# SwitchHead attention in a four-layer Trainium2 kernel: keys in four partition groups, probabilities turned by VectorE, gated values halved by GpSimd

## The reference, cut to what matters

```python
q = _rope(jnp.einsum('bsd,hdp->bhsp', x, Wq))        # 16 heads of 64
k = _rope(jnp.einsum('bsd,hdp->bhsp', x, Wk))
gv = _gate(x, Wsel_v)                                # 2 of 8 experts, sigmoid weights
v = jnp.einsum('bsd,bhse,hedp->bhsp', x, gv, Wv)
att = jax.nn.softmax(jnp.einsum('bhsp,bhtp->bhst', q, k) / np.sqrt(P), axis=-1)
o = jnp.einsum('bhst,bhtp->bhsp', att, v)
go = _gate(x, Wsel_o)
src2 = jnp.einsum('bhsp,bhse,hepd->bsd', o, go, Wo)
```

## Time and profile before

| | |
|---|---|
| median of 3 runs | 5357.71 us (5347.48 to 5360.96) |
| the profiled execution | 5350.9 us |
| its span, first to last instruction | 5349.1 us |
| mean granted TensorE clock | 0.966 |
| SwitchHead's score rows | 1062.5 to 3645.7 us of the span |

### The profile page before, as it was taken

The page is one execution under the profiler, slowest core; times in us unless marked ns, Lnnn a source line. Parts: engine busy times, 40 slices in busy tenths (PEclk is TensorE's granted clock), DMA queues, the critical chain, the costliest instruction groups (busy, mean ns, idle before and its releaser), DMA issues.

```text
span 5349.1 us, 83763 instructions
## 1 busy us (share of the span) xinstructions
PE 4801.0 (90%) x30340; PEld 2480.0 (46%) x30378; DVE 3571.9 (67%) x4077; ACT 2898.9 (54%) x3797; POOL 2348.7 (44%) x1499
## 2 busy tenths in 40 slices
PE   6989898689999999999999999997888988888856
PEld 2334333256556666565666556564333322222226
DVE  5899999866655565556655674654776778888721
ACT  5665556245445545555455554553555557667743
POOL 4888888535534543535534444443221221120014
PEclk8999999899999999999999999998999999999978
DMA  4555555323332332333323332233112101101005
GB/s 152 189 182 183 179 190 193 124 56 82 86 80 78 86 94 72 82 83 79 94 68 86 89 95 65 72 91 85 39 34 43 41 25 26 25 25 25 2 30 169
DMA packets 202377, 467.59 MB, mean 87 GB/s; under 512 B 35179, under 2 KB 52078, under 8 KB 201316
## 3 DMA queue, kind: packets, MB, share of 16 engines
q1 hardware_dynamic: 198968, 455.89, 29.9%
q0 software_dynamic: 3008, 6.32, 0.3%
HBM read 417.51 MB, written 33.99 MB: 84 GB/s over the span
## 4 chain that ended last, share of the span: by engine, by line
PE 72%; issue 9%; DVE 8%; ACT 6%; POOL 3%; DMA 0%; SPq 0%; POOLq 0%; DVEq 0%; ACTq 0%
PE ps L2258 8%; PE ps L1350 8%; PE ps L1370 8%; PE ps L1389 8%; PE ps L1358 7%; PE ps L1339 7%; PE ps L548 4%; PE ps L2229 3%; PE ps L2211 3%; ACT n_P L2293 3%; PE ps L495 2%; PE ps L1332 2%; DVE ps L713 1%; DVE n_MX L2372 1%; DVE m_HH L734 1%
## 5 line engine op out<-in xcount | busy, mean ns | idle before, releaser
L2372 DVE TENSOR_REDUCE n_MX<-ps 128x2 f32<-128x1024 f32 (+6 forms) x1034 | 982.2, 979 | 235.6 <-PE ps L2211 137.1
L1496 ACT ACTIVATE s_P<-ps,s_MX 128x1024 f32<-128x1024 f32 x512 | 570.4, 1114 | 968.1 <-DVE s_MX L1660 968.0
L2293 ACT ACTIVATE n_P<-ps 128x1024 f32<-128x1024 f32 (+4 forms) x1022 | 825.3, 838 | 447.2 <-PE ps L2229 233.7
L1652 DVE TENSOR_TENSOR XTB<-ps,s_GVJ 128x1024 f32<-128x1024 f32 x256 | 313.2, 1223 | 837.3 <-PE ps L1339 836.4
L771 POOL TENSOR_TENSOR m_PR<-m_HH,m_CS 128x1024 f32<-128x1024 f32 x256 | 605.9, 2381 | 156.2 <-issue 129.4
L1660 DVE TENSOR_REDUCE s_MX<-ps 128x1 f32<-128x1024 f32 x512 | 600.3, 1214 | 32.1 <-PE ps L1350 32.0
L1867 POOL TENSOR_TENSOR s_OG<-s_OG,s_OT 128x1024 f32<-128x1024 f32 x256 | 604.4, 2374 | 38.8 <-DMA s_OG<-s_gt 38.6
L1505 ACT ACTIVATE shared<-ps 128x1024 f32<-128x1024 f32 x512 | 496.7, 1023 | 140.0 <-PE ps L1358 138.4
L1350 PE MATMUL ps<-s_QF 64*128 64x512 f32 x2048 | 510.6, 617 | 28.1 <-POOL s_QF L1859 20.0
L1358 PEld LDWEIGHTS ps<-ident,s_P 128*128 128x128 f32 x4096 | 464.0, 141 | 150.5 <-issue 135.3
L1370 PEld LDWEIGHTS ps<-shared,s_V 128*64 128x64 f32 x8192 | 442.0, 137 | 197.4 <-issue 172.4
(11 more groups left out here) (352 smaller groups left out, 6484.7 us busy)
## 6 DMA issues: line engine op xcount, KB each, us to landing
m_CS<-m_rows_c SPq DMA_DIRECT2D x256, 512.0 KB
s_OG<-s_gt SPq DMA_DIRECT2D x512, 256.0 KB, 4.2
m_BS<-m_rows_c SPq DMA_DIRECT2D x80, 512.0 KB
s_WV<-in_s_v SPq DMA_DIRECT2D x32, 512.0 KB, 4.0
s_TA<-XTB SPq DMA_DIRECT2D x256, 64.0 KB, 2.3
s_WO<-in_s_o SPq DMA_DIRECT2D x32, 512.0 KB, 5.3
g_WB<-in_g_wx SPq DMA_DIRECT2D x23, 578.0 KB
n_parts<-n_PT SPq DMA_DIRECT2D x14, 768.0 KB, 3.4
```

The lines of the kernel that those rows point to most:

```text
L2293: ins = s.activation(P[:, at:at + x.shape[1], lo:512], x[:, :, lo:512], ACT.Exp, scale=scale)
L2372: ins = v.tensor_reduce(self.MX[:, q, at:at + x.shape[1], hp, t], x[:, :, 0:width], AX.X, ALU.max)
```

## The change

Scores are laid out anew. A tile's score block (128 queries x 1024 keys) becomes 32 matmuls in place of 4: for query group a (32 queries) and key group x (keys whose index has (k mod 128) // 32 = x), the result of 32 x 256 goes to partitions 32x to 32x+31 and columns 256a. With keys in the partitions' groups this way, a transpose in blocks of 32x32 is all that the probabilities need, and VectorE does it from SBUF to SBUF (`v.transpose`, 128x1024), in place of TensorE's transposes and ScalarE's copies.

A query's maximum and sum are then spread over four partition groups. ScalarE copies the scores to SBUF (`row`); VectorE takes maxima of 256 (`max`); SP gathers the four groups with four DMAs; VectorE reduces over them (`most`); SP sends the result to the four groups with four more; ScalarE takes eight exponentials of 256 columns per tile in place of two of 1024 (`exp`). At the end of a half SP gathers the sums with four DMAs, VectorE adds, inverts and transposes them (`recip`), SP stores them to DRAM (`spread`) and broadcasts them back with two DMAs (`over`), and GpSimd multiplies as before. The steps `turn` and `sums` leave TensorE and the ring of PSUM slots.

The sum over the 8 gated experts is split: GpSimd adds the upper four to the lower four (512 elements), and VectorE adds up the four that are left in a step of its own, `v_sum`, later in the turn. In a turn the order is now: gated, onto, recip, max, v (product, halving), exp of the tile before, its first transpose, most, its second transpose, v_sum, sums, spread, over, collect, values, keep, rope, ahead, qk, gate_in.

```diff
     NG = 3
-    NP = 4
+    NP = 6
...
-        self.MX, self.M1 = sb("MX", [128, 8]), sb("M1", [128, 64])
-        self.SU, self.SR, self.SX = sb("SU", [128, 2, 4, 2]), sb("SR", [128, 2, 4, 2]), sb("SX", [128, 4, 2, 64])
+        self.M1 = sb("M1", [128, 64])
+        self.MX, self.MB = sb("MX", [128, 2, 8]), sb("MB", [128, 2, 8])
+        self.MG, self.MR = sb("MG", [32, 2, 4, 8]), sb("MR", [32, 2, 8])
+        self.SU, self.SG, self.SR = sb("SU", [128, 2, 32]), sb("SG", [32, 4, 32]), sb("SR", [32, 3, 32])
...
-        self.PT = [self.TMP[:, u * 2048:(u + 1) * 2048].rearrange("p (h k n) -> p h k n", h=2, k=NT) for u in range(2)]
+        self.PT = [self.TMP[:, u * 2048:(u + 1) * 2048].rearrange("p (h n) -> p h n", h=2) for u in range(2)]
...
+        if m % 4 == 1 and due(5):
+            out.append(("recip", *self.of_half(m // 4 - 1)))
+        if due(0):
+            out.append(("max", *tile(0)))
+        if m == 2:
+            next(vs)
+            out.append(("v_sum", *out[-1][1:]))
+            begun = len(out)
+        next(vs, None)
+        if due(1):
+            out.extend([("exp", *tile(1), 0), ("exp", *tile(1), 1), ("turn", *tile(1), 0)])
+        if due(0):
+            out.append(("most", *tile(0)))
+        if due(1):
+            out.append(("turn", *tile(1), 1))
+        out.extend(("v_sum", *s[1:]) for s in [s for s in out[begun:] if s[0] == "v"])
+        if m % 4 == 0 and due(4):
+            out.append(("sums", *self.of_half(m // 4 - 1)))
+        if m % 4 == 1 and due(5):
+            out.append(("spread", *self.of_half(m // 4 - 1)))
+        if m % 4 == 2 and due(6):
+            out.append(("over", *self.of_half(m // 4 - 1)))
+        if due(self.GATED + 1) and part(self.GATED + 1)[1] == 3:
+            out.append(("collect", *self.of_half(part(self.GATED + 1)[0])))
+        if due(2):
+            g = m - 2
+            out.append(("values", *self.pair(g // 8), g % 8))
+            if g % 4 == 3:
+                out.append(("keep", *self.of_half(g // 4)))
...
-        if m % 4 == 0 and due(4):
-            out.append(("recip", *self.of_half(m // 4 - 1)))
-        for _ in range(2 if m == 2 else 1):
-            next(vs, None)
...
+            elif kind == "max":
+                g = self.tile(*step[1:])
+                sp.wait_ge(self.mx_done, g + 1)
...
+                for x in range(4):
+                    sp.dma_start(self.MG[:, g % 2, x, :], self.MX[32 * x:32 * x + 32, g % 2, :]).then_inc(self.mg_in, 16)
+            elif kind == "most":
+                g = self.tile(*step[1:])
+                sp.wait_ge(self.most_done, g + 1)
...
+                for x in range(4):
+                    sp.dma_start(self.MB[32 * x:32 * x + 32, g % 2, :], self.MR[:, g % 2, :]).then_inc(self.mb_in, 16)
+            elif kind == "sums":
+                k = self.half(*step[1:])
+                sp.wait_ge(self.exp_done, 8 * (k + 1))
...
+                for x in range(4):
+                    sp.dma_start(self.SG[:, x, :], self.SU[32 * x:32 * x + 32, k % 2, :]).then_inc(self.su_in, 16)
+            elif kind == "spread":
+                k = self.half(*step[1:])
+                sp.wait_ge(self.recip_done, 2 * (k + 1))
...
+                sp.dma_start(self.sums_d[k % 2], self.SR[:, 2, :]).then_inc(self.sums_out, 16)
+            elif kind == "over":
+                k = self.half(*step[1:])
+                sp.wait_ge(self.sums_out, 16 * (k + 1))
...
+                rows = self.sums_d[k % 2].rearrange("(t h a) q -> h t (a q)", t=4, h=2)
+                for h in range(2):
+                    sp.dma_start(self.OR[k % 2][64 * h:64 * h + 64, 1, :].rearrange("p (t n) -> p t n", t=4),
+                                 rows[h].partition_broadcast(64)).then_inc(self.or_in, 16)
...
-                for q in chunks(L):
-                    for h in range(2):
-                        hs = slice(64 * h, 64 * h + 64)
-                        ins = pe.matmul(r.ap(two[h])[:, q], QF[hs, 0, t * 128:(t + 1) * 128], QF[hs, 1, q], start=True, stop=True)
-                        if q.stop == L:
-                            ins.then_inc(*r.fill(two[h]))
-            elif kind == "turn":
-                P = self.P[self.head(step) % self.NP]
-                r.taken(pe, ("row", *step[1:]))
-                r.empty(pe, step)
-                for t in range(NT):
-                    ins = pe.transpose(ps[:, t * 128:(t + 1) * 128], P[:, t * 128:(t + 1) * 128], c.ident[:, :])
-                ins.then_inc(*r.fill(step))
...
+                        place = self.O[64 * h:64 * h + 64, 128 * (g % 4):128 * (g % 4) + 128].rearrange("p (a n) -> p a n", n=32)
+                        P = self.PT[g % 2][:, h, :].rearrange("p (a k n) -> p a k n", a=4, n=32)[:, :, i, :]
+                        ins = pe.matmul(place, self.V[j % 2][:, h, i, :], P, start=i == 0, stop=i == NT - 1)
...
             elif kind == "row":
-                g, x = self.tile(*step[1:4]), self.head(step)
-                s.wait_ge(self.mx_done, x + 1)
+                x = self.head(step)
+                r.filled(s, step)
                 if x >= self.NP:
-                    r.filled(s, self.old("turn", x - self.NP))
-                if g % 4 == 0 and g >= 8:
-                    s.wait_ge(self.recip_done, g // 4 - 1)
-                s.activation(self.P[x % self.NP][:, :], ps, ACT.Exp, bias=self.MX[:, x % 8:x % 8 + 1],
-                             accum_out=self.SU[:, g // 4 % 2, g % 4, step[4]:step[4] + 1]).then_inc(*r.take(step))
-            elif kind == "turn":
...
-                s.activation(self.PT[g % 2][:, step[4], :, :].rearrange("p k n -> p (k n)"), ps, ACT.Copy).then_inc(*r.take(step))
+                    s.wait_ge(self.pt_done, x - self.NP + 1)
+                s.activation(self.P[x % self.NP][:, :], ps, ACT.Copy).then_inc(*r.take(step))
+            elif kind == "exp":
+                g, x, h = self.tile(*step[1:4]), self.head(step), step[4]
+                if h == 0:
+                    s.wait_ge(self.mb_in, 64 * (g + 1))
+                    if g % 4 == 0 and g >= 8:
+                        s.wait_ge(self.su_in, 64 * (g // 4 - 1))
+                for a in range(4):
+                    P, at = self.P[x % self.NP][:, 256 * a:256 * a + 256], 8 * (g % 4) + 4 * h + a
+                    ins = s.activation(P, P, ACT.Exp, bias=self.MB[:, g % 2, 4 * h + a:4 * h + a + 1],
+                                       accum_out=self.SU[:, g // 4 % 2, at:at + 1])
+                ins.then_inc(self.exp_done, 1)
...
-                r.taken(v, step)
-                v.tensor_reduce(self.V[u][:, :, t, :], four(self.VP), AX.X, ALU.add).then_inc(self.v_done, 1)
-            elif kind == "row":
-                x = self.head(step)
-                r.filled(v, step)
-                if x >= 8:
-                    r.taken(v, self.old("row", x - 8))
-                v.tensor_reduce(self.MX[:, x % 8:x % 8 + 1], ps, AX.X, ALU.max, negate=True).then_inc(self.mx_done, 1)
+            elif kind == "max":
+                g = self.tile(*step[1:])
+                if g > 1:
+                    v.wait_ge(self.mg_in, 64 * (g - 1))
+                for h in range(2):
+                    x = self.head((*step, h))
+                    r.taken(v, ("row", *step[1:], h))
+                    ins = v.tensor_reduce(self.MX[:, g % 2, 4 * h:4 * h + 4],
+                                          self.P[x % self.NP][:, :].rearrange("p (a k) -> p a k", a=4), AX.X, ALU.max)
+                ins.then_inc(self.mx_done, 1)
+            elif kind == "v_sum":
+                t, u = step[3], j % 2
+                VP = self.VP.rearrange("p (h q e) -> p h q e", h=2, e=8)
+                v.wait_ge(self.halved, n(*step))
+                v.tensor_reduce(self.V[u][:, :, t, :], VP[:, :, :, 0:4], AX.X, ALU.add).then_inc(self.v_done, 1)
+            elif kind == "most":
+                g = self.tile(*step[1:])
+                v.wait_ge(self.mg_in, 64 * (g + 1))
+                if g > 1:
+                    v.wait_ge(self.mb_in, 64 * (g - 1))
+                v.tensor_reduce(self.MR[:, g % 2, :], self.MG[:, g % 2, :, :].rearrange("p x e -> p e x"), AX.X, ALU.max,
+                                negate=True).then_inc(self.most_done, 1)
+            elif kind == "turn":
+                g, x = self.tile(*step[1:4]), self.head(step)
+                v.wait_ge(self.exp_done, x + 1)
+                if g == 0:
+                    v.wait_ge(self.top_done, 1)
+                elif g > 1:
+                    v.wait_ge(self.values_done, g - 1)
+                v.transpose(self.PT[g % 2][:, step[4], :], self.P[x % self.NP][:, :]).then_inc(self.pt_done, 1)
             elif kind == "recip":
                 k = self.half(*step[1:])
...
-                v.reciprocal(self.SR[:, k % 2, :, :], self.SU[:, k % 2, :, :]).then_inc(self.recip_done, 1)
+                v.wait_ge(self.su_in, 64 * (k + 1))
```

(21 more changed lines are left out.)

99 lines of the change are left out of this document (47 added, 52 removed).

## The result

The changed kernel takes 5779.2 us (median of 4 runs, 5777.7 to 5789.4), the kernel before 5359.3 us beside it. The ratio is 1.079 with an interval of 1.077 to 1.081: 420 us slower, where 71 us slower were forecast. The profiled execution has a span of 5778.5 us.

A forecast was written before the change was run, and what follows sets the result against it. TensorE bounds the kernel before; after the change SP's queue would set the round, 10.05 us plus extras, 10.4 against 10.1. Over 256 turns +77 us; 5350.9 + 77 + 7 gives 5435, rounded to 5430; range 5160 to 5650.

The forecast's parts named there:

- The mechanism forecast first: SwitchHead's score stage: SP's issues and the trip inside its queue eat what the transposes gave; 5370 to 5530, chance 0.50.
- The rival of cheap issues: SP's small copies cost 0.3 us an issue, so TensorE binds with 8.6 to 9 us a turn; 5050 us, chance 0.13.
- that of dear transposes: An engine is dearer: VectorE block transposes of 2.44 us or scores at 3.8, a turn of 11.3; 5660 us, chance 0.17.
- the third, in which the extras overlap: Extras overlap better than the round-by-round maximum, so SP's 9.5 us a turn holds; 5180 to 5340 us, chance 0.20.
- One sign that the prediction named as speaking against it: Wait list naming ScalarE's exponentials or the copies' landing rather than SP's order would show the forecast wrong.
- TensorE's side of the sum: TensorE's turn in the stage: 10.1 less 1.75 and 0.1 for transposes, plus 0.4 for scores, 8.6 us (8.2 to 10.1).
- The 0.2 us a turn for GpSimd's `over`: GpSimd's `over` waits for the spread sums ahead of output gates and halving: 2 us late once in eight turns.
- the round itself: From one `max` issue to the next, the later of SP and VectorE per turn: sum 80.4, 10.05 us a turn.
- d=0: Turn 0 of the eight in a pair of heads: SP 10.0 us with the sums' gather, VectorE 9.4 with collect; so 10.0.
- three small instructions: `recip`'s work on VectorE, which makes its round 9.25 us in turns 1 and 5 of a pair of heads.
- I take ... 1.65 to land: Small DMAs of the maxima, 32 rows of 32 bytes: 1.65 us from issue to landing, lower bound 0.65.
- "0.15" for copies behind loads: Max copies queue behind gate loads and 0.8 MB of output weights and slots in SP's queue: 0.15 us a turn.

The follow-up runs named there:

- 3: Changed kernel without the maximum over the four partition groups: its eight DMAs a turn and `most` left out (output not the reference's); 5105.0 us, ratio 0.952.
- 8: Kernel before the change, with eight 32x8 copies a turn added on SP into memory nobody reads; 5354.8 us beside 5351.2, ratio 1.000.
- 10: Changed kernel with each gate load from the fourth on cut from 256 KB to 8 KB, number and place kept; 5706.4 us, ratio 1.066.
- 6: Changed kernel with SP issuing each turn's gate-load pair right behind the max copies, not behind the `most` copies; 5666.9 us, ratio 1.058.
- 12: Changed kernel with `recip` moved behind `v_sum` and gate loads cut from 512 columns to 16; 5643.7 us, ratio 1.055.
- 7: Changed kernel with GpSimd's halving taken out and `v_sum` summing all eight values on VectorE; 5773.4 us, ratio 1.079.
- 2: Changed kernel with the gate loads issued on ScalarE's DMA queue instead of SP's, behind the exponentials; 5891.1 us, ratio 1.099.
- 4: Changed kernel with `recip` behind `v_sum` and maxima moved between partition groups by VectorE and ScalarE copies, not DMAs; 5783.0 us, ratio 1.079.
- 5: Kernel of 4 with VectorE's four gathering copies written as reductions over an axis of one element; 5233.7 us, ratio 0.977.

## Why the prediction was right in sign and short in size

**What held.** The mechanism forecast first is the one that sets the time. SP's order of issues and the trip inside it took more than TensorE gave: 3 shows it by taking the trip away, 8 by issues without a trip. The terms of work held as well. An issue lasts 0.59 us (four in 2.41 or 2.46), the scores' pass 2.0 us (taken 2.3), the block transpose 1.23 (1.22), eight exponentials 202.9 / 51.5 = 3.9 (4.0 with their reads), `v_sum` 0.64 (0.68). No row had shown whether GpSimd holds up the block transposes: it doesn't, the 512 of them lasted 1.21 to 1.25 us. The rival of cheap issues and that of dear transposes are both refuted by their own rows, and the third, in which the extras overlap, by the table of rounds, of which none is shorter than its sum. One sign that the prediction named as speaking against it did appear, though: the waits of VectorE and ScalarE name the copies' landing first. It stands beside SP's order, not in its place, since both lie in the same chain. TensorE's side of the sum was near too: without the trip (3) its work is 8.4 us a turn, against the 8.6 worked out, and the turn 10.1 - 254 / 256 = 9.1. The 0.2 us a turn for GpSimd's `over` was not tried by itself. From 1500 to 2500 us VectorE waited for the halving for only 8.4 us in 86 turns, 0.1 a turn.

**What failed, in short.** The turn takes 11.7 us where 10.4 were forecast. The failed step is the round itself: a mean of 10.05 us, as the later of SP's and VectorE's queue, each summed by itself. In one round of eight a wait between the two was missing (the first point below), the copies' landing was set too low (the second), and SP's waits, pauses and long issues were set too low in all rounds (the third). The last is the largest: with the other two put right the time is still 213 us above the forecast.

**The step that failed first: d=0, "SP has the sums' gather ... 10.0; VectorE ... 9.4".** The two were summed apart and the later taken. But `recip`, on VectorE ahead of the next maxima, waits for that gather, so SP's gather, its landing and VectorE's maxima lie one behind the other. The prediction priced `recip` as "three small instructions" (9.25 - 8.7 = 0.55 us in d=1; they last 0.35 + 0.34 + 0.20 = 0.9) and never asked what it waits for, nor what is queued behind it. Measured, d=0 takes 14.09 us. Putting `recip` later takes 63 us off.

**The second: the landing, "I take ... 1.65 to land", with "0.15" for copies behind loads.** For the return copies 1.65 is right. The max copies follow 512 KB of gate data in every turn, not now and then, and land in 2.6. 10 and 6 show the cause from two sides, and its price is 73 us, 0.29 us a turn in place of 0.15. Since 0.15 a turn (38 us) was in the forecast, 35 us of the miss are due to it. The warning stood in the earlier trace rows: a gate load takes 4.2 us to land and was issued just ahead.

**The third, worked out and not tried by itself: the round's own sum.** 12 leaves 213 us above a forecast that still holds the 38 us for the landing: 251 us to explain, or 0.98 us a turn. SP's waits in it from 1500 to 2500 us (90 turns):

```profile
SPq L1221 <- DVE s_MR L1724: 156.1, 90, 5.3
SPq L1212 <- DVE s_MX L1711: 32.4, 32, 2.8
```

These are 188.5 / 90 = 2.1 us a turn, where the forecast's rounds had 1.85 (1.35 in the trip and 0.5 for VectorE). Of these the trip's part grew, to 156.1 / 90 = 1.7 us. Its median, over all turns but the first eight, is 1.4 us and so as forecast; the mean is higher because of single turns. The last of the four copies lands after 1.74 us in the median but after more than 3.1 us in a tenth of the turns, and in d=1 VectorE begins `most` only 1.1 us after the landing on average. Issues were forecast at 13.4 x 0.615 = 8.25 us. A turn of 11.2 us (without the first eight) then has some 0.85 us more, where the forecast had nothing but the 0.2 for `over`. SP's timeline gives where it lies: some three pauses a turn of 0.1 us between groups (0.3 in all), and one issue in every two turns that lasts over 0.8 us in place of 0.59 (0.4 us a turn; such a one is in the 3.52 for four, above). Together that is 0.25 + 0.85 - 0.2 = 0.9 of the 0.98 us, and the first eight turns, 28 us longer than eight others, hold about the rest. The pause could have been read in the earlier trace rows (1186.38 + 2.46 = 1188.84, and the next starts at 1188.94), and the earlier trace rows show a longest issue of 1728 ns. Why single copies land late and single issues are long stays open.

**Where doubt was priced wrongly.** The prediction gave 0.20 to extras that overlap better than a round-by-round maximum, and no case of its own to the opposite. A maximum over separately summed queues is a lower bound of the round, since every wait between two queues can only add to it. The range's upper end came from a dear transpose, not from the trip, which was the least known part.

**The halving** has no gain of its own in the forecast, and 7 finds none. But the forecast took VectorE for the later queue in four rounds of eight (d = 1, 3, 5 and 7), so the 0.6 us should have counted there, and it didn't: SP waited for the maxima in 28 of 86 rounds only. That is a second sign that the two queues, each summed by itself, do not give the round.

## What to carry to other kernels

A round trip of small DMAs inside an in-order queue is paid as a chain, not as so many issues: write down for each instruction in it what it waits for and what stands behind it, in one list over all queues. Small copies issued right behind large loads landed 0.9 us later, and the loads' size made the difference (10); moving the loads to another queue did not help (2). So put the large load where nobody waits behind it. If partition groups must exchange a few numbers, let a compute engine move them, and on VectorE by a reduction rather than a copy where GpSimd is at work: here the reduction in the copy's place turned 5783 us into 5234, from 8% slower to 2% faster than before.

## What the runs showed of the hardware

- A 1 KB copy within SBUF lands 1.7 us (median) after its issue begins, and 2.6 us where a pair of 256 KB loads was issued just ahead; with 8 KB loads in the same place it is 1.7 again.
- VectorE's copies of 32x8 took 0.16 to 2.3 us each beside a busy GpSimd, 0.76 on average (4); reductions that move the same data took 0.105 to 0.155 us (5), and ScalarE's copies of that shape a mean of 0.20 us (5).
- 64 matmul instructions of 64x32 weights by 256 columns took 2.0 us in all, though one lasts 389 ns on average: they overlap, at little loss against the 1.92 us of the eight 64x128 by 512 before.
- A block transpose of 128x1024 4-byte elements takes VectorE 1.23 us, about as long as its maxima (1.20) and its product with the gates (1.21) over as many elements.
